# Two quarters of a linear layer moved to two banks of the other PSUM set, one of them ahead of the gated factor's transposes, and the last layer's result kept and stored in place

## What is computed

```
for l in 0..3:
    y = cond_l(x, cond_512)      # four 3-tap convolutions: same, up, same, down
    x = x + ffn_l(y)             # y @ W_l + bias + a low-rank part
# low-rank part:
#   layer 0: a fixed factor            (folded into W)
#   layer 1: top 2 of 8 experts by the softmax of a router's logits, rank 16
#   layer 2: chosen by the sample      (folded into W)
#   layer 3: top 1 of 4 experts, rank 8
```

## Time and profile before

| | |
|---|---|
| median of 3 runs | 1207.51 us (1206.16 to 1208.16) |
| the profiled execution: its time | 1208.1 us |
| its span, first to last instruction | 1206.3 us |
| PE busy | 1172.3 us, 97% |
| DVE busy | 520.3 us, 43% |
| ACT busy | 349.8 us, 29% |
| POOL busy | 541.3 us, 45% |
| granted PE clock, mean over the span | 0.996 of full speed |

### The profile page before, as it was taken

One profiled execution on the slowest core, in us unless ns is written; L12 is line 12 of the kernel. 1 busy time (PEld: TensorE's weight loads), 2 busy tenths in 40 slices (PEclk: granted clock), 3 DMA queues, 4 the chain that ended last, 5 costly groups with the idle time before them and its releaser, 6 DMA issues.

```text
span 1206.3 us, 38332 instructions
## 1 busy us (share of the span) xinstructions
PE 1172.3 (97%) x17688; PEld 686.7 (57%) x17688; DVE 520.3 (43%) x1012; ACT 349.8 (29%) x634; POOL 541.3 (45%) x411
## 2 busy tenths in 40 slices
PE   5899999999999999999999999999999999999997
PEld 4345565555565555655555556555566565565565
DVE  6863443443343434343444343444343344434343
ACT  2253233233222223123322222323222223313221
POOL 4657524555435436444155553355354541654300
PEclk9899999999999999999999999999999999999999
DMA  5534100021313000002123000002112100001001
GB/s 151 231 137 173 40 2 2 2 63 71 142 60 118 2 2 2 2 6 94 72 72 134 10 2 2 2 2 98 72 48 82 50 2 2 2 1 72 2 19 53
DMA packets 21567, 63.30 MB, mean 52 GB/s; under 512 B 4672, under 2 KB 5376, under 8 KB 17184
## 3 DMA queue, kind: packets, MB, share of 16 engines
q1 hardware_dynamic: 19632, 60.13, 13.7%
q10 hardware_dynamic: 1776, 0.73, 0.3%
HBM read 43.02 MB, written 17.83 MB: 50 GB/s over the span
## 4 chain that ended last, share of the span: by engine, by line
PE 88%; DVE 4%; issue 0%; DMA 0%; ACT 0%; DVEq 0%
PE bank_b L1326 28%; PE bank_a L119 14%; PE bank_a L106 11%; PE bank_b L106 11%; PE bank_b L89 9%; PE bank_a L1263 5%; PE bank_b L1284 3%; PE bank_a L77 3%; PE bank_b L1278 2%; PE bank_b L1338 2%; PE bank_b L1319 1%; DVE z L1169 1%; PE bank_b L1297 1%; PE bank_b L1307 1%; PE bank_b L1340 1%
## 5 line engine op out<-in xcount | busy, mean ns | idle before, releaser
L934 POOL TENSOR_TENSOR sum_v<-raw_v 128x768 f32<-128x768 f32 x30 | 55.3, 1844 | 552.8 <-ACT raw_v L993 552.8
L1326 PE MATMUL bank_b<-w_hi,y3t_hi 128*128 128x512 f32 x512 | 208.4, 407 | 0.0
L1326 PE MATMUL bank_b<-w_hi,y3t_lo 128*128 128x512 f32 x512 | 202.5, 395 | 0.0
L1326 PE MATMUL bank_b<-w_lo,y3t_hi 128*128 128x512 f32 x512 | 202.0, 394 | 0.0
L119 PE MATMUL bank_a<-y,w_down 64*32 64x512 f32 x3072 | 172.2, 590 | 0.0
L1119 DVE TENSOR_TENSOR x<-bank_b,x 128x512 f32<-128x512 f32 x96 | 66.4, 692 | 180.0 <-PE bank_b L1326 140.2
L986 ACT ACTIVATE y<-bank_a,cb,tab 128x512 f32<-128x512 f32 x64 | 49.6, 776 | 314.6 <-PE bank_a L119 309.2
L106 PE MATMUL bank_a<-y,wv 32*64 32x512 f32 (+2 forms) x3584 | 138.1, 476 | 0.8 <-issue 0.8
L106 PE MATMUL bank_b<-y,wv 32*64 32x512 f32 (+2 forms) x3584 | 137.2, 476 | 0.0
L1326 PEld LDWEIGHTS bank_b<-w_hi,y3t_hi 128*128 128x128 f32 x512 | 96.6, 189 | 35.1 <-issue 13.4
L89 PE MATMUL bank_b<-xs,cw 32*32 32x512 f32 x3072 | 111.9, 611 | 2.7 <-DVE var L553 1.9
(11 more groups left out here) (194 smaller groups left out, 1444.1 us busy)
## 6 DMA issues: line engine op xcount, KB each, us to landing
w_hi<-w_scratch SPq DMA_DIRECT2D x9, 1024.0 KB, 5.3
w_lo<-w_scratch SPq DMA_DIRECT2D x9, 1024.0 KB, 8.0
x_in<-in_x SPq DMA_DIRECT2D x32, 256.0 KB, 4.2
out_x<-out_tile SPq DMA_DIRECT2D x32, 256.0 KB, 2.3
w_raw<-in_w SPq DMA_DIRECT2D x3, 1024.0 KB, 6.4
w_scratch<-w_hi SPq DMA_DIRECT2D x3, 1024.0 KB, 4.2
w_scratch<-w_lo SPq DMA_DIRECT2D x3, 1024.0 KB, 7.1
w_raw<-w_scratch SPq DMA_DIRECT2D x2, 1024.0 KB, 9.9
```

What stands on the lines that cost most here:

```text
L934: ins = g_.tensor_tensor(dst[:, :, at:at + count].rearrange("p r k o -> p r (k o)"), src[:, :, 0:count].rearrange("p r k o -> p r (k o)"), ...
L1326: ins = pe.matmul(lin_ps[b][:], y3t[yi][:, k, P * b:P * (b + 1)], w[use(m) % 2][wi][:, k], start=(k == 0 and i == 0), stop=(k == KB - 1 an ...
```

## The change

`lin_ps` now gives quarters 2 and 3 banks 2 and 3 of bank_a. `linear_back` puts quarter 2 ahead of `adapter_turn` and splits quarter 3: three of its four slices of W stand where quarter 2 stood, the last one stays where quarter 3 was. New waits: `linear_back`, and plain phases ahead of quarter 2, wait until the second half of conv2 has been read out of bank_a (`y2_ends`); the second half of `down` waits for the residual of all four quarters, since it writes the banks of quarters 2 and 3. A wait for `w_sum_ready` in two of eight phases goes. The last layer's result is added in place into x and stored from there, so that DVE waits for no store; instead POOL waits, before x is overwritten with the next group, until the store of that quarter has landed (`stored`, now one semaphore for each group of the pair and quarter).

```diff
--- before.py
+++ after.py
@@ -754,21 +754,20 @@
     w_raw, w_sum = keep["w_raw"], keep["w_sum"]
     w = [[sb(f"w{u}_{part}", [P, KB, LEN], F32R) for part in ("hi", "lo")] for u in range(2)]
 
-    out_tiles = [sb(f"out_tile{u}", [P, LEN]) for u in range(2)]
     ident = keep["ident"]
 
     bank_a, bank_b = keep["bank_a"], keep["bank_b"]
     z_ps, logit_ps = bank_b[0], bank_b[1]
     zt_ps = logit_ps
 
-    lin_ps = [bank_b[2], bank_b[3], bank_b[0], bank_b[1]]
+    lin_ps = [bank_b[2], bank_b[3], bank_a[2], bank_a[3]]
 
     x_loaded = keep["x_loaded"]
     adapters_loaded = sem("adapters_loaded")
     w_raw_loaded, w_hi, w_lo, w_kept = (sem(n) for n in ("w_raw_loaded", "w_hi", "w_lo", "w_kept"))
     eff_done, w_sum_ready = sem("eff_done"), sem("w_sum_ready")
     w_loaded = [sem(f"w_loaded{u}") for u in range(2)]
-    stored = [sem(f"stored{u}") for u in range(2)]
+    stored = [[sem(f"stored{g}_{b}") for b in range(ROWS)] for g in range(2)]
     xs_ready, xb_ready, c2_done, dn_done = (keep[n] for n in ("xs_ready", "xb_ready", "c2_done", "dn_done"))
     tr_done = sem("tr_done")
     c0_done, pr_done, w2s_ready, v_sums, wv_ready, raw_ready, ghosts_ready, y0_act, y0_dve = (
@@ -907,9 +906,10 @@
                 if m >= 0 and layer(m) == LAYERS - 1:
                     for b in range(ROWS):
                         sp.wait_ge(x_ready, tiles(m, b + 1))
-                        sp.dma_start(io["out"][group(m)][:, b], out_tiles[b % 2][:]).then_inc(stored[b % 2], 16)
-            for u in range(2):
-                sp.wait_ge(stored[u], 16 * GROUPS * 2)
+                        sp.dma_start(io["out"][group(m)][:, b], x[m % 2][:, b]).then_inc(stored[m % 2][b], 16)
+            for g in range(2):
+                for b in range(ROWS):
+                    sp.wait_ge(stored[g][b], 16 * ITERS)
 
         @block.gpsimd
         def _(pool):
@@ -957,8 +957,8 @@
                                                 ALU.subtract).then_inc(w_lo, 1)
                 if l < LAYERS - 1:
                     for b in range(ROWS):
-                        if l == 0 and n >= 2:
-                            pool.wait_ge(x_ready, tiles(n - 2, b + 1))
+                        if l == 0 and n >= STEP:
+                            pool.wait_ge(stored[g][b], 16 * (n // STEP))
                         nc.gpsimd.tensor_tensor(x[g][:, b], src[:, b], keep["ob"][:, l], ALU.add).then_inc(xb_ready, 1)
                 if n + 1 < PHASES:
                     scaled_weights(n + 1)
@@ -1110,13 +1110,7 @@
                 dve.wait_ge(lin_done, tiles(m, b + 1))
                 if l < LAYERS - 1:
                     dve.wait_ge(xb_ready, biased(m, b + 1))
-                    result = x[g][:, b]
-                else:
-                    result = out_tiles[b % 2][:]
-
-                    if group(m) or b >= 2:
-                        dve.wait_ge(stored[b % 2], 16 * (2 * group(m) + b // 2))
-                v.tensor_tensor(result, lin_ps[b][:], x[g][:, b], ALU.add).then_inc(x_ready, 1)
+                v.tensor_tensor(x[g][:, b], lin_ps[b][:], x[g][:, b], ALU.add).then_inc(x_ready, 1)
 
             def wide(small, e):
                 return small[:].unsqueeze(2).broadcast_to((P, ROWS, e))
@@ -1250,6 +1244,8 @@
 
             def down(n, u):
                 pe.wait_ge(y2_ends, 2 * n + 2)
+                if u:
+                    pe.wait_ge(x_ready, tiles(n - 1, ROWS))
                 if n + 1 < PHASES:
                     pe.wait_ge(raw_ready, evacuated(n + 1))
                     pe.wait_ge(ghosts_ready, evacuated(n + 1))
@@ -1319,9 +1315,9 @@
                     ins = pe.transpose(zt_ps[0:rows, P * t:P * (t + 1)], z[:, t, 0:rows], ident[:])
                 ins.then_inc(zt_done, 1)
 
-            def base(m, b):
+            def base(m, b, ks=range(KB)):
                 l = layer(m)
-                for k in range(KB):
+                for k in ks:
                     for i, (yi, wi) in enumerate(PASSES):
                         ins = pe.matmul(lin_ps[b][:], y3t[yi][:, k, P * b:P * (b + 1)], w[use(m) % 2][wi][:, k],
                                         start=(k == 0 and i == 0), stop=(k == KB - 1 and i == 2 and l in (0, 2)))
@@ -1350,13 +1346,16 @@
                 else:
                     pe.wait_ge(w_loaded[u % 2], 32 * loads(u))
 
-            def linear_back(m):
+            def linear_back(m, convolve):
+                if convolve:
+                    pe.wait_ge(y2_ends, 2 * (m + 1) + 2)
+                base(m, 2)
                 adapter_turn(m)
-                base(m, 2)
+                base(m, 3, range(KB - 1))
                 pe.wait_ge(zt_ready, before(m, (1, 3)) + 1)
                 for b in range(3):
                     adapted(m, b)
-                base(m, 3)
+                base(m, 3, range(KB - 1, KB))
                 adapted(m, 3)
 
             def summed(m):
@@ -1383,11 +1382,10 @@
                 if n + 1 < PHASES:
                     products(n + 1)
                 if adapts:
-                    linear_back(m)
+                    linear_back(m, convolve)
                 else:
                     base(m, 1)
-                    if m % STEP in EFF:
-                        pe.wait_ge(w_sum_ready, summed(m) + 2)
+                    pe.wait_ge(y2_ends, 2 * n + 2)
                     base(m, 2)
                     base(m, 3)
                     effective(m, 1)
```

## The result

| | before | after |
|---|---|---|
| median of 4 runs each, one beside the other | 1207.63 us (1206.16 to 1208.16) | 1198.94 us (1197.62 to 1200.82) |
| ratio, 95% interval | | 0.9929 (0.991 to 0.9948) |
| the profiled execution: time, span | 1208.1, 1206.3 us | 1199.32, 1197.1 us |

What follows compares the result with a forecast made beforehand. PE, busy 1172.3 of 1206.3 us, was taken as the bound, so only its waits pay. Stall 8.16 plus run-out 0.5 less change of kind 1.4 gives 7.3 us, hence 1200.2 us; range 1198.3 to 1203.6.

Steps and rivals of the forecast that it cites:

- The stall: In eight layer-1 phases PE's transposes of the gated factor wait for DVE's z; removing 1.02 us each gains 8.16 us.
- The change of kind: On PE, quarter 2 (fp32r) directly behind products (fp32) costs 0.10 us more in 14 phases, 1.4 us in all.
- the upper bound of 2.8 us: Cost of the change of kind if the step into the transposes costs as much again: twice 1.4 us.
- the change would be free: Rival: quarter 2's weights are in place before products end, no cost; gain 8.7 us, time 1198.8; chance 0.06.
- The run-out: In the last two phases a smaller stall goes and the last residuals end earlier: together 0.5 us gained.
- The cover for the turned factor: PE work between transposes and low-rank part falls from 3.29 to 2.59 us; slack 0.57 us left, cost 0.
- Down's wait and POOL's: Down's second half waits for four residuals (slack 1.3 to 2.3 us), POOL's adds for stores; both cost 0.
- The check on PE's waits: Sign: the transposes' line on z is gone, and no line for the low-rank part on zt replaces it.
- the late factor: Rival: PE stops at zt_ready in sixteen gated phases; at 0.25 us each 4 us lost, 1204.2; chance 0.08.
- the slower case: Rival: down's second half stops for residuals in 31 phases; with 0.35 us a phase 1211.1; chance 0.05.
- the change shortens nothing: Rival: PE waits at conv0 for xs instead of for z; all 8.16 us back, 1208.4; chance 0.07.

Runs made afterwards that it cites:

- The run with the split in the middle: Changed kernel with quarter 3 split in the middle, six matmuls instead of nine as cover for the turned factor; 1204.44 us, ratio to before 0.9978.
- the run with early products: Changed kernel with products ahead of quarter 1 in gated phases, right behind the transposes of z and the logits; 1231.99 us, ratio to before 1.0224.

## Why the prediction was right, step by step

- *The stall* (8.16 us in eight phases): right. The line is gone, and the time from products to quarter 2 is the 1.37 us that the prediction took from layer 3. The old order on the new banks has it back, which shows that the order of the work is the cause.
- *The change of kind* (14 x 0.10 = 1.4 us): the term that was mis-sized. Its place was right: quarter 2's first step behind products is 0.34 us instead of 0.23. But the four transposes now follow matmuls of the linear layer at the usual step (0.23 us, so the upper bound of 2.8 us was not needed), and from their start to quarter 3 it is 174.32 - 173.97 = 0.35 us, where it was 0.42. Net, a layer-1 phase got 0.98 us shorter instead of 0.92, and a layer-3 phase 0.05 longer instead of 0.10: some 0.6 us instead of 1.4. The prediction looked only at the new neighbour of quarter 2 and not at that of the transposes. By the Trainium skill's "TensorE: Matmul & The Clock Gate", section "Step-by-step: what each phase is for", as the prediction read it, the change would be free and the time 1198.8; the measured 1198.94 is nearer to that. But the rows don't show it free: the first step has its 0.1 us, and another place gives most of it back.
- *The run-out* (0.5 us): right in its sum, once the drop of the clock in before's execution is set aside, but with some luck: the last residual ends 0.7 us earlier after the last conv0 (55.2 instead of 55.9), and from its end to the end of the span 2.95 us pass instead of 2.74, a term that the prediction did not have.
- *The cover for the turned factor*: right to 0.01 us. 0.57 us of slack were left, and the run with six matmuls shows what happens when it is used up.
- *Down's wait and POOL's* at no cost: right, no line of PE's waits and no phase shows one. The wait half a down earlier shows the slack of 1.4 us in layer 3 by taking it.
- *The check on PE's waits* was too weak. The prediction would have read "no line for the low-rank part" as "no stall". The run with the split in the middle has no line and loses 0.3 us a phase.

Of the rivals, the late factor and the slower case were each made to happen, and cost 5.5 and 31 us beside the changed kernel's time; in the changed kernel itself neither occurs. That the change shortens nothing is ruled out by the eight layer-1 phases; PE does not wait for xs at conv0 in any phase. Of the 8.7 - 7.3 = 1.4 us, 0.8 are the change of kind; the other 0.6 lie within the spread of the runs, and the drop of the clock that before's median can hold, 1.56 us, is larger than that. That the time came out 1.3 us from the forecast thus says less for the working than the phases do.

## What to carry to other kernels

A stall of an engine that is busy 97% of the time is removed by other work that can stand in it, and often the only thing that forbids this is where that work's result lies; so look for a free bank before looking for a faster producer. Before moving an instruction, follow what its consumers' consumers do at the new time: products moved by one quarter set POOL going beside DVE, and two or three of DVE's twenty steps of 0.19 us grew about tenfold. Read starts, not idle time: a stall shorter than a row is not in the list of waits, and it costs more than its length.

## What the runs showed of the hardware that was not expected

- A DVE step of 0.19 us became 1.57 to 2.16 us beside a POOL sum, only where both of its inputs lie in SBUF. In the changed kernel the last such step of the gate (L1157) ends at 171.12, 1.1 us before POOL's first sum starts at 172.22; z itself, which ends at 172.04, reads PSUM and would not be held up.
- A wait that PE finds met costs little, but not nothing: with one more of them ahead of the transposes, PE started 0.15 instead of 0.06 us after z, in all nine phases that have the wait, and 0.06 in the one that doesn't. A matmul that stood 0.18 us is followed by a step of 0.33 instead of 0.23.
- PE's long stalls cost more than their time. In the run with early products PE stood for 3.29 us in five phases, and in three of them the granted clock fell to half, once within the stall (at 218.1) and twice when PE had been at work again for 0.4 and 0.9 us (at 757.4 and 511.7). It stayed there for 3.4 to 6.8 us while the work went on:

```profile
218.00:225.00 7.00, 5.57 (x15) 4.55 (x16) 2.03 (x6) 0.60 (x1) 0.41 (x1) 0.51 0.00 0
```

```profile
219.43 1.11 PE L1315 MATMUL bank_b<-ident,z 128*128 128x128 f32 x4 [3.29 <-DVE z L1163]
...
221.20 0.63 PE L1322 MATMUL bank_a<-w_hi,y3t_lo 128*128 128x512 f32 x1
221.62 0.63 PE L1322 MATMUL bank_a<-w_hi,y3t_hi 128*128 128x512 f32 x1
```

At 1.2 GHz a step is 0.43 us instead of 0.23. These three phases took 45.67 to 46.65 us, the two with the same stall and the full clock 44.1. The run's times spread with it: the mean granted clock is 0.992 in the fastest execution, 1223.45 us, and 0.981 in the longest, 1243.84. Before the change stalls of 1 us in layer 1 never did this in the phases of the two profiled executions. Whether the fall comes is not settled by the stall's length alone, as the five equal ones show; what else decides it stays open.
